# Dealing the independent matmuls of an attention block to its sixteen steps in another order

## What is computed

```python
ln = layernorm(latents)                 # latents: the normalized 8 x 512 x 512 input
xn = layernorm(ctx)                     # 8 x 120 x 384
q  = ln @ Wq.T
kv = concatenate([xn @ Wkv.T, ln @ Wlkv.T], axis=1)    # 120 + 512 = 632 keys
k, v = kv[..., :512], kv[..., 512:]     # 8 heads of 64
qn, kn = rmsnorm(q) * SCALE, rmsnorm(k)
attn = softmax(where(mask, qn @ kn.T, -max))
x1 = x + tanh(g) * ((attn @ v) @ Wo.T + bo)
```

## Time and profile before

| | |
|---|---|
| median of 3 runs | 4306.66 us (4304.27 to 4310.42) |
| the profiled execution, its own time | 4306.23 us |
| its span | 4304.5 us |
| PE busy | 3971.2 us, 92% of the span |
| DVE, ACT, POOL busy | 69%, 46%, 23% |
| first attention, to the last output product | about 1112 us from the span's start |

### The profile page before, as it was taken

How to read it: one execution, slowest core, us unless ns; L and a number is a source line. 1 busy time by engine, 2 the same in 40 slices (tenths; PEclk the granted TensorE clock), 3 DMA queues, 4 the chain that set the end, 5 groups by cost and what they waited for, 6 DMA issues and landing times. The chain is left out here.

```text
span 4304.5 us, 68747 instructions
## 1 busy us (share of the span) xinstructions
PE 3971.2 (92%) x23968; PEld 3205.2 (74%) x23968; DVE 2977.4 (69%) x4625; ACT 1978.6 (46%) x2806; POOL 1003.8 (23%) x1012
## 2 busy tenths in 40 slices
PE   5999999998589999999987998967999999999998
PEld 3665555564379999999983555547999999999998
DVE  3766666666467667667643788757888888877885
ACT  3655555554144444444422544514444444444443
POOL 3211122210011101101103666403222223322221
PEclk9999999999699999999998999968999999999999
DMA  2000000000166666665632122106766666666664
GB/s 91 22 32 30 30 17 24 28 20 20 59 216 205 208 209 205 208 210 198 208 125 72 45 93 79 40 29 209 212 213 208 214 207 214 209 215 209 211 211 125
DMA packets 376608, 578.80 MB, mean 134 GB/s; under 512 B 25960, under 2 KB 186792, under 8 KB 376488
## 3 DMA queue, kind: packets, MB, share of 16 engines
q1 hardware_dynamic: 344024, 503.50, 35.2%
q0 software_dynamic: 26208, 61.68, 5.7%
q10 hardware_dynamic: 6256, 12.06, 0.8%
HBM read 518.31 MB, written 58.86 MB: 134 GB/s over the span
## 5 line engine op out<-in xcount | busy, mean ns | idle before, releaser
L1111 DVE TENSOR_TENSOR e_WL<-e_raw,e_WH 128x2048 fp32r<-128x2048 f32 x418 | 957.1, 2290 | 474.0 <-ACT e_WH L1060 470.3
L1060 ACT ACTIVATE e_WH<-e_raw 128x2048 fp32r<-128x2048 f32 x418 | 798.8, 1911 | 798.1 <-PE bank L1038 570.3
L1022 PE MATMUL bank<-e_xh,e_WH 128*128 128x256 f32 x3968 | 1126.9, 284 | 38.5 <-ACT e_hf L1076 19.0
L1022 PE MATMUL bank<-e_xl,e_WH 128*128 128x256 f32 x3968 | 1126.2, 284 | 0.0
L1022 PE MATMUL bank<-e_xh,e_WL 128*128 128x256 f32 x3968 | 1126.1, 284 | 0.0
L1022 PEld LDWEIGHTS bank<-e_xh,e_WH 128*128 128x128 f32 x3968 | 765.3, 193 | 42.0 <-issue 28.4
L1022 PEld LDWEIGHTS bank<-e_xl,e_WH 128*128 128x128 f32 x3968 | 765.4, 193 | 2.3
L1022 PEld LDWEIGHTS bank<-e_xh,e_WL 128*128 128x128 f32 x3968 | 765.0, 193 | 0.0
L1038 PE MATMUL bank<-e_WH,e_hh 128*128 128x512 f32 x1360 | 534.9, 393 | 0.0
L1038 PE MATMUL bank<-e_WH,e_hl 128*128 128x512 f32 x1360 | 529.7, 389 | 0.0
L1038 PE MATMUL bank<-e_WL,e_hh 128*128 128x512 f32 x1360 | 529.0, 389 | 0.0
(11 more groups left out here) (216 smaller groups left out, 6131.3 us busy)
## 6 DMA issues: line engine op xcount, KB each, us to landing
e_raw<-in_w SPq DMA_DIRECT2D x262, 1024.0 KB, 5.2
e_raw<-in_w SPq DMA_DIRECT2D x312, 512.0 KB
y<-e_Yo ACTq DMA_DIRECT2D x23, 512.0 KB, 2.9
a_X<-in_x SPq DMA_DIRECT2D x32, 256.0 KB, 2.6
a_R<-in_x SPq DMA_DIRECT2D x32, 256.0 KB, 4.0
x<-a_R SPq DMA_DIRECT2D x32, 256.0 KB, 2.0
a_X<-x SPq DMA_DIRECT2D x32, 256.0 KB, 3.4
x<-a_X SPq DMA_DIRECT2D x32, 256.0 KB, 2.0
```

The lines of the kernel that those rows point to most:

```text
L1022: mm = nc.tensor.matmul(up[n % RING][:, q * ROWS:q * ROWS + ROWS], w, x[:, c, :], start=(c == 0 and i == 0), stop=(c == DC - 1 and i == 2))
L1060: act.activation(WH[:, p, :], raw[:, s, :], ACT.Copy).then_inc(high_ready.sem, 1)
L1111: dve.tensor_tensor(WL[:, p, :], raw[:, p % 2, :], WH[:, p, :].bitcast(F32), ALU.subtract)\
```

## The change

The fills are dealt to other steps, and the steps of `SUM_AT` and `SCALE_AT` follow. `v` 3 and `v` 2 move to the end of the order: `v` 2 to step 15, and `v` 3 to step 0 of the next body, where it belongs to the batch whose softmax is then under way. The body in which `v` 3 is computed, the index of its input and output, and the waits for it change with that.

```diff
-FILLS = ((("tr", 0),), (("pv", 3), ("q", 0)), (("o", 0), ("o", 1)), (("o", 2), ("k", 0)),
-         (("o", 3), ("v", 0), ("tr", 1)), (("pv", 0),), (("q", 1), ("k", 1), ("tr", 2)), (("v", 1), ("q", 2)),
-         (("k", 2), ("tr", 3), ("tq", 0), ("tk", 0)), (("pv", 1), ("v", 2), ("tq", 1), ("tk", 1)), (("q", 3),), (("k", 3), ("tr", 4), ("tq", 2), ("tk", 2)),
-         (("v", 3), ("k", 4)), (("pv", 2),), (("v", 4), ("tq", 3), ("tk", 3)), (("tk", 4),))
+FILLS = ((("tr", 0), ("v", 3)), (("pv", 3),), (("o", 0), ("o", 1)), (("o", 2), ("q", 0)),
+         (("o", 3), ("k", 0), ("tr", 1)), (("pv", 0),), (("v", 0), ("q", 1), ("tr", 2)), (("k", 1), ("v", 1), ("tq", 0), ("tk", 0)),
+         (("q", 2), ("k", 2), ("tr", 3)), (("pv", 1),), (("q", 3), ("tq", 1), ("tk", 1)), (("k", 3), ("tr", 4)),
+         (("k", 4), ("tq", 2), ("tk", 2)), (("pv", 2),), (("v", 4), ("tq", 3), ("tk", 3)), (("v", 2), ("tk", 4)))
 FILL_ORDER = [f for step in FILLS for f in step]
-SUM_AT = {4: 0, 7: 1, 9: 2, 12: 3, 13: 4}
-SCALE_AT = {5: 0, 8: 1, 10: 2, 13: 3, 14: 4}
+SUM_AT = {5: 0, 8: 1, 9: 2, 12: 3, 13: 4}
+SCALE_AT = {6: 0, 9: 1, 11: 2, 13: 3, 14: 4}
 STATS_AT = {5: (0,), 8: (1,), 10: (2,), 12: (3,), 14: (4,)}
 NORM_AT = {6: (0,), 9: (1,), 11: (2,), 13: (3,), 15: (4,)}
@@ there
+            if f == ("v", 3):
+                return 0 <= b < B
+        v_body = lambda n, t: n if t == 3 else n - 1
@@ tensor
-                            pe.wait_ge(xl_ready, QT * (b + 1) + t + 1)
+                            pe.wait_ge(xl_ready, QT * (b if f == ("v", 3) else b + 1) + t + 1)
-                            wait_emptied(pe, bb - 1, ("v", kt))
+                            wait_emptied(pe, v_body(bb, kt), ("v", kt))
@@ scalar
-                        i = act.activation(V[0:rows, (b + 1) % 2, t, :], m[0:rows, :], ACT.Copy)
+                        i = act.activation(V[0:rows, (b if t == 3 else b + 1) % 2, t, :], m[0:rows, :], ACT.Copy)
@@ vector, columns
-                        wait_filled(dve, b - 1, ("v", t + 2))
+                        wait_filled(dve, v_body(b, t + 2), ("v", t + 2))
```

## The result

The changed kernel takes 4273.51 us, median of 4 runs (4271.42 to 4274.54), against 4306.94 us before. The ratio is 0.9921, with a 95% interval of 0.9904 to 0.9938: 0.8% faster. The forecast was 4272.0. The profiled execution has a span of 4269.7 us.

A forecast was written before the change was run, and what follows sets the result against it. PE was taken as the bound wherever a step has enough fills. Savings of 26.1 (bodies 1 to 6) + 3 + 0.8 + 4.5 = 34.4 off 4306.2 gave 4271.8, a median of 4272, range 4262 to 4282.

The forecast's parts named there:

- The price list: Prices from full steps: projection 2.81 us, scores with transposes 2.50, transpose group 0.44, context projection 2.58; empty step's floor 4.87.
- One sign given ahead: Profile after: step 10 would be the only one that got much longer, its mask 3.2 us after its scores.
- step 7: 9.00 us of work plus 0.3 while `tk` 0 waits for the copy of `v` 1: 9.3, old 8.12.
- step 12: 5.96 us of work; DVE enters with `scale` 2 and `norm` 2, lag 0.5: 6.44, old 7.89.
- The start: Body -1, which loses `v` 3: 4.5 us less, the middle of bounds 2.8 and 6.5.
- the walk: Following each wait of body -1, from transpose to projection: 6.5 us less.
- Body 0: First body, without `pv` 3 and `o`: 110.1 against 114.15, 4.0 less; 3 kept for a possible half-rate stretch.
- Behind body 6: Body 7: only `v` 3 in step 0, 0.8 more; step 1 at full clock; about 0.8 us less in all.
- (c): Rival: PE's clock still drops in front of each body, 1.7 x 8 = 14 us, 4286; chance 0.09.
- (b): Rival: on the shared port POOL's bias additions delay more L558, 20 us given back, 4292; chance 0.08.
- (a): Rival: waits inside steps 7, 10, 12 and 15 mostly absent, 23 us more won, 4249; chance 0.09.
- (d): Rival: clock drops several times a body, in holes of steps 10, 12, 14, 15; at four, 4320; chance 0.02.
- (e): Rival: nothing changes because DVE bounds steps 8 to 15; 4300 to 4310; chance 0.04.

## Why the prediction was right

**The price list.** Steps 1, 8, 9, 10 and 14 were forecast at 7.43, 8.55, 7.43, 7.71 and 7.18, and body 2 shows 7.43, 8.54, 7.43, 7.72 and 7.18. Step 0 (5.78), step 11 (5.65 forecast, 5.64) and step 15 (6.9, 6.87) are as close. The unchanged steps kept their length. One sign given ahead was too narrow: step 10 is not the only one that got much longer, since steps 7 and 15 grew by 1.3 and 1.15, as the forecast's own sum had them. A body was forecast 4.35 shorter; bodies 1 to 6 are 24.64 / 6 = 4.11 shorter.

**The difference, 0.24 a body,** is a net. Bodies 1 to 5 take 123.5 for the 123.1 forecast, and body 6, whose steps 10, 12 and 14 are shorter (7.26, 6.21 and 6.72), takes 122.66. The 0.4 lies in steps 7 and 12. In step 7 the wait of `tk` 0 was taken as 0.3, and the step takes 0.46 over its 9.00 of work. In step 12 the lag was taken from `scale` 2 and `norm` 2 alone; the two additions of POOL in step 11 hold up one L562 there, and 6.71 to 6.76 was measured for 6.44. The experiment with the additions in step 7 gives 6.38.

**The start** was given 4.5, the middle of 2.8 and 6.5; 7.31 came, above the upper bound. The 6.5 of the walk was the better value. The half-rate stretch that halved my estimate came, 3.4 us long, but before it was 6.8 long.

**Body 0** was given 3 and brought 0.6. I allowed one stretch at half rate, 1 us; steps 1 to 3 took 19.74 for the forecast 15.52. In steps 2 and 3, 2.8 of the 4.2, the mechanism was named and its length was not: the clock stayed at half from 108.3 to 118.6, through the nearly empty step 2 and into step 3. The rest is step 1, which was taken as an empty step of 4.87. It takes 6.01 at full clock in the kernel with tk 4 first: DVE does `columns` there and starts the mask 2.17 after the scores, and ACT keeps the order of a step with a `pv`, so PE waits 3.22 for the copies of the large transposes. By chance step 0 makes up for it, at 4.66 for the forecast 5.78, because in body 0 it has no probabilities to transpose. The stretch at half rate is no constant of the deal. With only the order of step 15 changed (tk 4 first) it was 3.4 us, body 0 took 111.0, 3.1 less than before, and the first scores came at 101.28, 4.4 earlier than before. The two terms together, 7.5, fit both kernels (7.9 and 7.5); how they divide hangs on where the clock falls, which the sum did not see.

**Behind body 6** 0.8 was forecast and 2.6 came; step 1 fell from 8.96 to 7.43 as said, and other steps of body 7, where nothing is left to fill, vary with the clock: in the seven kernels made from the changed one this part takes 127.2 to 130.9, against 129.03 before. So most of the 2.6 is chance. The errors have opposite signs: +2.8, -2.4, +1.8, -1.5 and, behind the stage, -0.4 make the sum right to 0.4 us of the profiled execution, the fastest of the four, and to 1.5 us of the median. That it is so near is luck of 3 us or so; the 24.6 for 26.1 in bodies 1 to 6 is not.

**The rivals.** (c), a clock that still drops in front of a body, is out: step 0 reads 1.00. (b), the port, is partly there, as 0.3 us in step 12: no further instruction was caught, but the two L558 (now L562) that were long in steps 10 and 11 of body 2 before, 0.78 and 1.51, now take 1.15 and 1.51, and the experiments showed what it costs where it meets a lag: 1.7. (a) is not in this kernel, but was there to be had: the wait in step 15 is worth 1.1 a body and the one in step 7 another 0.4. (d) and (e) are out.

**What was not seen** is how the parts share the gain. The sum went step by step and took the new deal as a whole. Step 0 grew by 0.2 in the mean and step 15 by 1.2 for two projections of 2.81 us, which the other steps no longer hold: 5.6 less 1.4 leaves 4.2 a body, and 4.11 was measured. The even deal of the middle is neutral alone; beside the filled edge it avoids one step so empty that the clock falls.

## What to carry to other kernels

In a software pipeline cut into steps, take the price of each piece of work from steps that are full, and the floor from a step that is empty; then the length of every new step can be written down ahead of time, here to a few hundredths of a microsecond where only such prices entered, and to 0.3 where a wait had to be guessed. Work was nearly free only in steps below the floor, so look first for pieces that can cross a loop's edge into them; evening out steps above the floor gained nothing here. Within a step, issue first the piece whose copy others wait for, and after every move look at what the slow helper engine will now run beside.

## What the runs showed of the hardware

- A bias addition of POOL and these DVE instructions hold each other up: a 128x632 `tensor_scalar` took 1.51 instead of 0.55, a 128x512 one 1.49 instead of 0.54, the cast 1.47 instead of 0.43, a two-input 128x1024 multiplication 1.96 instead of 1.21, and two additions took 3.69 instead of 2.54. The mask and the maxima, which read PSUM, kept their 0.41 and 0.81 beside the additions (most plainly in the kernel with the additions in step 9: a mask of 0.41 at 410.13 and two maxima in 1.54 at 410.57, inside the additions of 409.85 to 415.29). The Trainium skill, "SBUF — State Buffer", section "Who interferes with whom", names both kinds, two-port modes and two SBUF inputs; the traces agree for both.
- PE's clock was granted at half, 1.2 GHz, in step 0 after 2.68 us of idle time in step 15. It stayed at 2.4 GHz through idle times of 1.3 in step 10 and 1.06 in step 15. With step 15 filled and 1.8 us of idle time in step 0, it fell in step 1 in two bodies of six: identical bodies, one with the drop and one without. The same with only the edge changed: behind 1.99 us of idle time in step 11 (1.62 and 0.37) it fell in three bodies of six.
